# One decoder kernel, three reorderings: a context product in cross-attention, bias sums in a mixture of experts, VectorE's order in a delta rule

## The reference, cut to what matters

```
# 1. layer 0, cross-attention, 16 heads of 64: the queries are the 512 rows of x,
#    keys and values are 544 rows: the 512 of x and the 32 of the context
w   = softmax((q/8) @ k.T)                      # [512, 544] per head
out = concat_heads(w @ v) @ Wo
# 2. layer 0, feed-forward: 4 experts chosen by a remainder of floor(router)
ff = sum_e where(idx == e, relu(x @ W1[e] + b1[e]) @ W2[e] + b2[e], 0)
# 3. layer 1, gated delta rule (a scan over the tokens), 16 heads of 8
S = a_t * S;  S = S + k_t (b_t (v_t - S k_t))^T;  o_t = S q_t
```

## Time and profile before

| | us |
|---|---|
| median of 3 runs (lowest, highest) | 1846.54 (1839.44, 1847.07) |
| the profiled execution's own time | 1845.25 |
| its span, first to last instruction | 1843.4 |
| outside the span | 1.85 |
| PE busy | 1653.6 (90%) |
| DVE busy | 1271.4 (69%) |
| ACT busy | 949.4 (52%) |
| POOL busy | 304.5 (17%) |

### The profile page before, as it was taken

How to read it: one execution, slowest core, us unless ns; L and a number is a source line. 1 busy time by engine, 2 the same in 40 slices (tenths; PEclk the granted TensorE clock), 3 DMA queues, 4 the chain that set the end, 5 groups by cost and what they waited for, 6 DMA issues and landing times.

```text
span 1843.4 us, 24921 instructions
## 1 busy us (share of the span) xinstructions
PE 1653.6 (90%) x8074; PEld 736.0 (40%) x8074; DVE 1271.4 (69%) x2994; ACT 949.4 (52%) x2053; POOL 304.5 (17%) x465
## 2 busy tenths in 40 slices
PE   7899999999999989999899988444798899999998
PEld 3355455545544432222244331222443355444443
DVE  7576666767667768888565578999666677762423
ACT  3565556556645516666633566333236366664333
POOL 1000000000001021121277200000000222114443
PEclk9999999999999989999999999777799799999999
DMA  4000000000000220240000000000100512100000
GB/s 193 1 1 1 1 1 1 1 1 1 1 1 21 55 59 23 73 116 2 1 0 1 0 1 1 1 1 1 69 1 1 147 55 73 32 2 1 1 0 23
DMA packets 19806, 44.36 MB, mean 24 GB/s; under 512 B 3872, under 2 KB 13024, under 8 KB 18912
## 3 DMA queue, kind: packets, MB, share of 16 engines
q1 hardware_dynamic: 19200, 42.39, 7.6%
q10 hardware_dynamic: 480, 0.39, 0.1%
HBM read 32.74 MB, written 9.44 MB: 23 GB/s over the span
## 4 chain that ended last, share of the span: by engine, by line
PE 75%; DVE 16%; ACT 5%; issue 3%; POOL 1%; DMA 0%; ACTq 0%; POOLq 0%; SPq 0%; DVEq 0%
PE ps L675 8%; PE ps L639 8%; PE ps L653 6%; PE ps L1226 6%; PE ps L1264 5%; PE ps L1112 5%; PE ps L1699 3%; PE ps L1700 3%; PE ps L596 3%; PE ps L1596 3%; PE ps L1612 3%; PE ps L1707 3%; DVE arena L2063 2%; PE ps L684 2%; DVE arena L2050 2%
## 5 line engine op out<-in xcount | busy, mean ns | idle before, releaser
L1390 DVE TENSOR_REDUCE stat<-ps 128x1 f32<-128x512 f32 (+3 forms) x512 | 279.1, 581 | 86.6 <-PE ps L1116 43.0
L1321 ACT ACTIVATE arena<-ps 128x512 f32<-128x512 f32 (+3 forms) x512 | 247.1, 515 | 154.3 <-PE ps L1264 83.3
L826 DVE TENSOR_REDUCE stat<-ps 128x1 f32<-128x544 f32 x256 | 173.4, 719 | 163.0 <-PE ps L639 163.0
L777 ACT ACTIVATE arena<-ps,stat 128x544 f32<-128x544 f32 x256 | 180.7, 711 | 201.9 <-DVE stat L826 201.9
L1264 PE MATMUL ps<-arena 75*128 75x512 bf16 (+1 forms) x480 | 163.1, 344 | 11.7 <-ACT arena L1321 9.5
L1112 PE MATMUL ps<-arena 72*128 72x128 bf16 (+1 forms) x480 | 163.0, 348 | 8.0 <-DVE stat L1390 7.8
L675 PE MATMUL ps<-arena 128*64 128x512 f32 (+1 forms) x640 | 159.2, 609 | 4.7 <-DVE arena L845 3.3
L639 PE MATMUL ps<-arena 64*128 64x272 f32 x1024 | 152.1, 415 | 5.1 <-ACT arena L777 4.3
L785 ACT COPY arena<-ps 128x512 f32<-128x512 f32 x256 | 137.3, 594 | 15.5 <-PE ps L653 15.5
L653 PEld LDWEIGHTS ps<-wA_sb,arena 128*128 128x128 f32 x1024 | 115.1, 142 | 70.1 <-issue 68.9
L653 PE MATMUL ps<-wA_sb,arena 128*128 128x128 f32 x1024 | 138.3, 278 | 0.0
(11 more groups left out here) (391 smaller groups left out, 2775.2 us busy)
## 6 DMA issues: line engine op xcount, KB each, us to landing
arena<-b_parts SPq DMA_DIRECT2D x180, 96.0 KB
b_parts<-arena SPq DMA_DIRECT2D x64, 128.0 KB, 1.9
reg<-wM_dram SPq DMA_DIRECT2D x1, 3072.0 KB, 10.0
reg<-wB_dram SPq DMA_DIRECT2D x1, 2048.0 KB, 12.4
reg<-wM_dram SPq DMA_DIRECT2D x1, 2048.0 KB, 16.7
reg<-wD_dram SPq DMA_DIRECT2D x1, 1817.0 KB, 10.7
wF_sb<-wF_dram SPq DMA_DIRECT2D x1, 1476.0 KB, 19.8
reg<-b_parts SPq DMA_DIRECT2D x12, 96.0 KB
```

The costliest lines, as they stand in the source:

```text
L777: e.activation(prob_of(P, r).rearrange("p (a k) -> p a k", a=2), score_banks(r), ACT.Exp, bias=x_neg[:, at_:at_ + 1], accum_out=x_sums[:, ...
L826: e.tensor_reduce(x_neg[:, n % 4:n % 4 + 1], score_banks(r), AX.XY, ALU.max, negate=True).then_inc(sem("max_done"), 1)
L1321: e.activation(p_t[:, m % 8, q0:T], ps[:, S1 + m % S2, q0:T], ACT.Exp).then_inc(exp_done, 1)
L1390: e.tensor_reduce(nm[:, G % 2, u // 4, u % 4:u % 4 + 1], ps[:, step % S1, 0:keys(u)], AX.X, ALU.max, negate=True).then_inc(max_done, 1)
```

## The change

It has four parts. (1) The context product of a pair moves from the start of TensorE's step `r` = 1 (behind that step's scores) to the end of step `r` = 0, right behind the value products 2 and 3; VectorE's `pv_read` moves ahead of the two maxima in step `r` = 1; the transpose on line 658 takes 128 columns instead of 64 and writes all of bank 6's partitions (rows 64 to 127 are read by nobody). (2) SyncE waits for the splits of batches 0 and 1 as well as for `pv_done` before the DMAs of line 1520. (3) `total(b)` of the experts waits for the last up matmul, adds the four masked biases, and adds PSUM last, after the last down matmul. (4) In the delta rule VectorE makes `u` first, then `ke` and `z`; `q` moves ahead of the second and third product, `q k` behind the two solves; the dots stand after 2 picks of `ke` instead of 5; the numbers of `READY` follow that order.

```diff
-                    e.transpose(ps[0:2 * S, 6, q * 128:q * 128 + 128], x_prob[:, P % 3, T:T + 2 * S],
+                    e.transpose(ps[:, 6, q * 128:q * 128 + 128], x_prob[:, P % 3, T:T + 128],
...
-                    if r == 1:
-                        if 0 <= (i - 9) // 4 < XP:
-                            pv((i - 9) // 4, (4,))
...
                     if r == 0 and 0 <= (i - 8) // 4 < XP:
                         pv((i - 8) // 4, (2, 3))
+                        pv((i - 8) // 4, (4,))
...
+                    if r == 1 and 0 <= (i - 9) // 4 < XP:
+                        pv_read((i - 9) // 4)
                     if i < XPAIRS:
                         neg_max(i, 0)
                         neg_max(i, 1)
-                    if r == 1 and 0 <= (i - 9) // 4 < XP:
-                        pv_read((i - 9) // 4)
...
                             if a and early is not None:
                                 e.wait_ge(sem("pv_done"), XP)
+                                e.wait_ge(split_q, 8)
+                                e.wait_ge(split_k, 8)
...
                 def total(b):
+                    e.wait_ge(sem("moe_up"), (b + 1) * NI)
+                    e.wait_ge(sem("masks"), b + 1)
+                    for ex in range(E0):
+                        link(e, e.scalar_tensor_tensor(out=x_aux[:, b, :], in0=mask[:, b % 2, ex, :], scalar=v("f_b2", ex),
+                                                       in1=x_aux[:, b, :], op0=ALU.mult, op1=ALU.add))
                     e.wait_ge(sem("moe_down"), (b + 1) * NI)
...
+                    e.tensor_tensor(x_aux[:, b, :], ps[:, 4 + b % 2, :], x_aux[:, b, :], ALU.add).then_inc(sem("b3_sum"), 1)
...
-            KE_FIRST = 5
+            KE_FIRST = 2
-            READY = {x: n_ + 1 for n_, x in enumerate(("gamma", "ke", "gq", "q0", "w", "u", "q1", "q2", "q3"))}
+            READY = {x: n_ + 1 for n_, x in enumerate(("gamma", "ke", "gq", "w", "u", "q0", "q1", "q2", "q3"))}
...
-                e.wait_ge(sem("b4_ready"), READY["gamma"])
-                e.tensor_tensor(g_ke, g_k, g_to_end, ALU.mult).then_inc(sem("b4_ready"), 1)
                 e.wait_ge(sem("b4_act_read"), 2)
-                link(e, e.tensor_tensor(g_z, g_k, g_beta, ALU.mult))
                 e.wait_ge(sem("b4_proj"), 4 * B)
                 e.scalar_tensor_tensor(out=split_i(g_u), ...)
                 e.wait_ge(sem("b4_ready"), READY["gamma"])
+                e.tensor_tensor(g_ke, g_k, g_to_end, ALU.mult).then_inc(sem("b4_ready"), 1)
+                link(e, e.tensor_tensor(g_z, g_k, g_beta, ALU.mult))
...
-                e.wait_ge(sem("b4_rlen"), 2 * B)
-                e.tensor_tensor(split_i(g_q), tokens_by_i(ps[:, 0:B, :]),
-                                split_i(r_q), ALU.mult).then_inc(sem("b4_dve_read"), 1)
+                    if s_ == 1:
+                        e.wait_ge(sem("b4_rlen"), 2 * B)
+                        e.tensor_tensor(split_i(g_q), tokens_by_i(ps[:, 0:B, :]),
+                                        split_i(r_q), ALU.mult).then_inc(sem("b4_dve_read"), 1)
...
-                e.tensor_tensor(g_pq[0], g_q, g_k, ALU.mult).then_inc(sem("b4_ready"), 1)
                 e.wait_ge(sem("b4_prod"), BL - 1)
...
+                e.tensor_tensor(g_pq[0], g_q, g_k, ALU.mult).then_inc(sem("b4_ready"), 1)
+                e.wait_ge(sem("b4_ready"), READY["q0"])
```

More of the change, by code:

```diff
@@ L1636, in total @@
                 def total(b):
-                    e.wait_ge(sem("moe_down"), (b + 1) * NI)
-                    e.wait_ge(sem("masks"), b + 1)
-                    link(e, e.tensor_tensor(x_aux[:, b, :], ps[:, 4 + b % 2, :], x_aux[:, b, :], ALU.add))
-                    for ex in range(E0):
-                        i = e.scalar_tensor_tensor(out=x_aux[:, b, :], in0=mask[:, b % 2, ex, :],
-                                                   scalar=v("f_b2", ex), in1=x_aux[:, b, :], op0=ALU.mult, op1=ALU.add)
-                        if ex < E0 - 1:
-                            link(e, i)
-                    i.then_inc(sem("b3_sum"), 1)
+                    e.wait_ge(sem("moe_up"), (b + 1) * NI)
[3 more added lines that the diff above has]
+                                                       in1=x_aux[:, b, :], op0=ALU.mult, op1=ALU.add))
+                    e.wait_ge(sem("moe_down"), (b + 1) * NI)
+                    e.tensor_tensor(x_aux[:, b, :], ps[:, 4 + b % 2, :], x_aux[:, b, :], ALU.add).then_inc(sem("b3_sum"), 1)
                 masks(e, 1)
```

## The result

| | kernel before | changed kernel |
|---|---|---|
| median of 10 runs, us | 1845.92 | 1856.34 |
| lowest, highest | 1839.44, 1853.33 | 1852.53, 1868.70 |
| span and granted clock of the profiled execution | 1843.4, 0.957 | 1866.8, 0.953 |

The changed kernel is slower: ratio 1.0065, 95% interval 1.0046 to 1.0084. Predicted were 1857.8 us (range 1846 to 1866), with "slower 0.55" among the chances, slower meaning by over 0.5%; the interval only just leaves 1.005 out. The medians lie 10.4 us apart where +11.3 was forecast. That agreement is better than the working deserves. One term, the delta rule, was wrong by more than 2 us, and smaller misses made up for it. The rest of this document takes the sum apart.

A forecast was written before the change was run, and what follows sets the result against it. TensorE, busy 90% of the span, was taken as the bound, with VectorE bounding the delta rule. Terms 13.3 + 0.8 + 0 - 2.8 = +11.3 us on the median 1846.54 gave 1857.8 us, range 1846 to 1866.

The forecast's parts named there:

- `r` = 0, 30 pairs: Cross-attention step that receives the context product: already full on TensorE (4.12 us), so it grows by 1.00 per pair.
- `r` = 1: Cross-attention step that gives the product away: 4.28 us falls only to 3.53, giving back 0.75 in most pairs.
- `r` = 2: Next cross-attention step: ScalarE's late read of bank 7 delays projection `q`, +0.21 with a values' copy, +0.33 with an `Ln`.
- behind the loop: Last two pairs, after step 127: the moved product delays VectorE's maxima or GpSimd's split, +0.8 us (0 to +1.5).
- experts: Last batch's sum ready earlier: -0.3 us, or +0.3 if a collision delays GpSimd's last mask; taken as 0.
- delta rule: VectorE-bound stage, new order: waits ahead of the first solve and the scan shrink, -2.8 us, or -2.0 if TensorE's clock falls.
- the floor of 3.53: Cross-attention: the loop of scores, maxima, exponentials and next scores keeps any step from lasting less than 3.53 us.
- the output steps: Three cross-attention pairs with the output projection at the end of `r` = 1: no floor met, that step shrinks by 1.07.
- Small loss: Rival, cross-attention: waits in `r` = 2 absorbed or the product cheaper, total +5 to +7 or +1, 1848 to 1854 us; chance 0.25.
- The 1.71 go: Delta rule: VectorE's idle 1.71 us before the first solve, waiting for the dots, disappears.
- the rivals: Small loss 0.25; context product nearly free (1840.7 us) 0.10; clock in favour 0.10; clock against 0.05.
- The clock: Two rivals, TensorE's clock in the loop: falls vanish, 1851 us, chance 0.10; falls once per pair, 1902 us, chance 0.05.

The follow-up runs named there:

- e1: Kernel before with only the moved context product, sums read ahead of the maxima, wide transpose and SyncE's waits: 1859.61 us, ratio 1.0072.
- e7: Changed kernel with ScalarE's read of bank 7 moved ahead of the two copies at the end of `r` = 1: 1851.25 us, ratio 1.0048 to the kernel before.
- e2: Kernel before with only the changes to the experts and to the delta rule: 1845.49 us, ratio 0.9998.
- e3: Kernel before with only the change to the delta rule: 1847.71 us, ratio 1.0014.
- e4: Changed kernel with the sums read behind the maxima again, context product left at its new place: 1876.33 us, ratio 1.0159 to the kernel before.
- e5: Kernel before with the changes to experts and delta rule, but 4 picks of `ke` ahead of the dots instead of 2: 1842.80 us, ratio 0.9997.
- e6: Kernel before with the changes to experts and delta rule, but 5 picks of `ke` ahead of the dots instead of 2: 1844.10 us, ratio 1.0003.
- e9: Kernel before in its own order, with 2 instead of 5 picks of `ke` ahead of the dots and nothing else: 1844.75 us, ratio 1.0007.

## Why the prediction was right, and where it was not

| term | predicted | measured | from |
|---|---|---|---|
| `r` = 0, 30 pairs | +30.0 | +30.1 | steps of the changed kernel, e1, e7 |
| `r` = 1 | -22.7 | -23.0 | the same |
| `r` = 2 | +6.0 | +5.4 | changed kernel, e1; gone in e7 |
| behind the loop | +0.8 | 0 to +0.8 | e1: gone 16 us behind the transposes; e7: still there |
| experts | 0 | -0.5 | e2 against e3 |
| delta rule | -2.8 | -0.1 to -0.7 | the changed kernel, e2, e3, e4, e7 |
| sum | +11.3 | +11.3 to +12.7 | ratio: +12.0 (8.5 to 15.5); medians: +10.4 |

**The context product** was right, step by step. The product cost 1.00 at its new place, not 0.86; `r` = 1 ended at the floor of 3.53 and gave back 0.75; the output steps gave 1.17 (6.86 to 5.69), where I had 1.07. Reaching the floor was what mattered, and e4 shows that without the earlier read it would not have been reached. The Trainium skill (TensorEngine Tiling (Array Packing), Key Properties) states that a change of the tiling mode drains TensorE. The trace agrees with what the prediction took from it, the same cost at both places: 1.00 and 1.00.

**The waits in `r` = 2** were right in place and nearly in size: +0.20 for a values' copy (0.21 predicted, 12 times) and +0.30 for an `Ln` (0.33, 10 times). "Small loss" as a rival needed them to be absorbed; they were not. e7 takes them away by the cause that I had named, and 5.4 us of the loop with them.

**Behind the loop** the delay came. Whether it lasts is open: e1 and e7 say opposite things, and their falls of the clock differ. The prediction showed who is late (VectorE) but did not follow it to a point at which that lateness ends the stage.

**The experts.** The -0.3 that I had written down and then rounded to nothing was -0.5. By the Trainium skill (SBUF — State Buffer, SBUF: two separate sides) VectorE with two SBUF inputs and a GpSimd instruction that reads SBUF exclude each other, and the later one waits. The trace agrees with 4.21 and 2.73. What I had derived from it, +0.3 by a late last mask, did not come: the mask started before the second bias, took its 1.26, and the bias was the one to wait.

**The delta rule is the step that failed.** The prediction put it so: "The 1.71 go", and, as a lesser case, "If TensorE's clock falls in the 2 us before the dots, they take up to 1.7 more, and 0.8 of that shows: -2.0." Everything up to the dots' start came as computed, to 0.2 us. But the clock did fall, in each of the five profiled executions with 2 picks and the new order, and the dots took 2.5 to 3.1 us more, of which 2.1 to 2.7 showed at the scan. I had priced the fall by stretches of 3.40 us at half clock, 1.7 lost; here 5.0 to 6.2 us of the dots' time ran in it. And I had given it no chance of its own, although my own working had put 3 picks out of the place ahead of the dots, which leaves TensorE idle there. e5 and e6 show the sum to be right once that place is filled: 47.15 against 47.1 predicted. e9 shows, in one execution, that the gap is enough without the new order. What decides exactly whether the clock falls I can't tell: e5 kept full clock through gaps of 2.01 and 1.64, e2 lost it in a gap of 3.99 behind the same 2.01, and the changed kernel and e3 lost it behind the 2.01 already. In the kernel before the fall came too, but in the 8 instructions that sum `q` (5.28 for them in the earlier trace rows, 3.60 in the changed kernel), which nobody was waiting for.

So the forecast of the total came this close by luck, since its errors cancel: 2.1 to 2.7 too much gain in the delta rule, against 0.7 too much loss in the loop, 0 to 0.8 behind it and 0.5 in the experts. None of the rivals took place. The clock neither helped nor hurt per pair; the added gaps of 0.35 and 0.46 in a loop whose other steps are full kept 1.00.

## What to carry to other kernels

Work moved from one step of a loop to another costs its full length where the step is full, and gives back only what lies above the floor that the other engines set: find that floor in a step that already has less work, before anything is moved. Follow every read that the shorter step leaves behind, since it becomes late in the next one; here it cost 5.4 us and one swap in ScalarE's order took it back. And where an edit opens a gap ahead of work that another engine waits for, price that work at half clock, or leave something in the gap: with two picks put back the stage was 2.1 to 2.7 us shorter in every profiled execution, though the time of the whole kernel did not show it.

## What the hardware showed that I had not expected

The same twelve matmuls took 5.42 us in six profiled executions, with at most 1.66 us of idle time ahead of them, and 7.11 to 8.48 in six others, with 2.90 to 3.99. That looks like one rule, but is not: in four of the six the clock fell in that idle time or behind it, in the other two ahead of it, 0.9 us into work that followed an idle time of 2.01; and seven more executions passed the same 2.01 at full clock. Untouched code is not of one length either: the stage from the scan's start on took 715.9 to 728.3 us, the larger differences where stretches at 0.50 differ. A total that moves by less than half a per cent says little about an edit here. The lengths of steps and of short stages say more, to 0.1 us where the clock is the same.
